# A batch's last pair in the second attention is attended one step later, and its outputs are turned in the next batch's second step

## The reference

```python
q = ln(x @ Wq + bq)                 # 16 heads of 16, 256 queries for each batch
k = ln(y_main @ Wk + bk); v = y_main @ Wv + bv      # 240 keys
k_dca, v_dca = ...                  # 16 more keys, from other weights
ctx = softmax(q k^T / 4) v + softmax(q k_dca^T / 4) v_dca   # two softmaxes, added
x = x + tanh(g_xattn[2]) * (ctx @ Wo + bo)
```

## Time and profile before

| | |
|---|---|
| median of three runs | 1056.01 us |
| the profiled execution | 1059.89 us |
| its span, first to last instruction | 1058.6 us |
| TensorE busy | 936.7 us (88%) |
| VectorE busy | 725.1 us (68%) |
| ScalarE busy | 520.7 us (49%) |
| GpSimd busy | 302.5 us (29%) |
| the steps of the second attention | about 705 to 867 us of the span |

### The profile page before, as it was taken

How to read it: one execution, slowest core, us unless ns; L and a number is a source line. 1 busy time by engine, 2 the same in 40 slices (tenths; PEclk the granted TensorE clock), 3 DMA queues, 4 the chain that set the end, 5 groups by cost and what they waited for, 6 DMA issues and landing times.

```text
span 1058.6 us, 14861 instructions
## 1 busy us (share of the span) xinstructions
PE 936.7 (88%) x4790; PEld 669.3 (63%) x4790; DVE 725.1 (68%) x1877; ACT 520.7 (49%) x1346; POOL 302.5 (29%) x284
## 2 busy tenths in 40 slices
PE   7878789999999999999999989877589988979667
PEld 3323334567999998888977767754355655545455
DVE  5899894245777677678676445576978965576764
ACT  4665672135666666566653434354346552123331
POOL 3767692121111112155101324234232200010210
PEclk8878899999999999999999999999899999989789
DMA  9500001001111164113103446312100003211201
GB/s 363 228 0 0 1 0 50 1 30 45 35 41 46 45 236 153 31 62 94 46 1 119 147 133 191 128 65 60 51 1 1 2 1 141 78 46 31 87 1 41
DMA packets 28500, 75.00 MB, mean 71 GB/s; under 512 B 4092, under 2 KB 5382, under 8 KB 27656
## 3 DMA queue, kind: packets, MB, share of 16 engines
q1 hardware_dynamic: 24344, 63.81, 17.6%
q0 software_dynamic: 3072, 8.39, 2.5%
q10 hardware_dynamic: 1008, 1.86, 0.6%
HBM read 52.03 MB, written 22.02 MB: 70 GB/s over the span
## 4 chain that ended last, share of the span: by engine, by line
PE 62%; DVE 15%; ACT 3%; issue 3%; DMA 1%; SPq 1%; POOL 1%; another core or an unknown queue 0%; DVEq 0%; POOLq 0%; ACTq 0%
PE psum L2195 5%; PE psum L1071 5%; PE psum L1796 5%; PE psum L1277 4%; PE psum L1288 4%; PE psum L927 4%; PE psum L1257 4%; PE psum L1268 2%; PE psum L938 2%; PE psum L1810 2%; PE psum L1095 2%; PE psum L2214 2%; PE psum L2816 2%; PE psum L2458 2%; DVE arena L2492 2%
## 5 line engine op out<-in xcount | busy, mean ns | idle before, releaser
L1167 POOL TENSOR_TENSOR arena<-arena,mhalf 128x8 f32<-128x8 f32 x32 | 53.4, 1670 | 232.6 <-DVE arena L1144 232.6
L1389 DVE SCALAR_TENSOR_TENSOR X<-psum,arena,X 128x256 f32<-128x256 f32 x128 | 56.0, 479 | 64.9 <-PE psum L1288 64.9
L455 POOL TENSOR_TENSOR arena<-arena 128x512 f32<-128x512 f32 x64 | 82.2, 1307 | 8.6 <-PE psum L545 5.1
L855 DVE TENSOR_TENSOR_SCAN arena<-psum,arena 128x512 f32<-128x512 f32 x64 | 74.8, 1210 | 7.9 <-ACT psum L711 6.8
L1331 ACT ACTIVATE arena<-psum,arena 128x256 f32<-128x256 f32 x128 | 59.9, 477 | 35.9 <-DVE arena L1368 33.5
L1796 PE MATMUL psum<-arena 128*128 x248 | 66.6, 391 | 10.6 <-DVE arena L1891 8.8
L2477 ACT ACTIVATE arena<-psum,arena 128x240 f32<-128x240 f32 x128 | 57.4, 463 | 32.3 <-DVE arena L2491 16.4
L545 PE MATMUL psum<-arena,ident 128*128 128x512 f32 x128 | 69.4, 669 | 0.1
L1288 PE MATMUL psum<-arena 128*128 128x256 f32 x256 | 65.9, 380 | 1.2 <-DVE X L1389 1.1
L1257 PE MATMUL psum<-arena 128*128 128x256 f32 x256 | 65.8, 380 | 0.0
L1277 PE MATMUL psum<-arena 128*128 128x256 f32 x256 | 65.8, 380 | 0.0
(11 more groups left out here) (367 smaller groups left out, 2255.7 us busy)
## 6 DMA issues: line engine op xcount, KB each, us to landing
arena<-in_w SPq DMA_DIRECT2D x32, 384.0 KB, 3.1
tokens<-arena SPq DMA_DIRECT2D x2, 4096.0 KB, 22.8
arena<-tokens SPq DMA_DIRECT2D x32, 256.0 KB
results<-arena SPq DMA_DIRECT2D x32, 256.0 KB
arena<-in_moe SPq DMA_DIRECT2D x17, 384.0 KB, 3.1
arena<-in_moe SPq DMA_DIRECT2D x4, 1536.0 KB, 12.8
arena<-in_w SPq DMA_DIRECT2D x2, 1024.0 KB, 6.1
arena<-in_gu SPq DMA_DIRECT2D x1, 1280.0 KB, 7.2
```

The costliest lines, as they stand in the source:

```text
L455: nc.gpsimd.tensor_tensor(m.HC[:, v, :], m.Hs[:, v, :], m.Cs[:, s % 2, :], ALU.mult).then_inc(*tick("HC", s, c))
L855: nc.vector.tensor_tensor_scan(m.Hs[:, 2 * (s % 2) + c, :], bank[m.bank_dA[c]], input_of(m, s, c), 0.0, ALU.mult, ALU.add).then_inc(*tick( ...
```

## The change

The loops are reordered around a batch's end. `attend(s - 1)` now runs in every step but the first, and never twice; only the very last pair is attended after the loop. The copies OSa and OSv move from g = 7 to the next batch's g = 0, behind PTa and PTv (on VectorE ahead of the maxima). `turned` moves from g = 0 to g = 1 and stands ahead of the scores; `normalised` moves to g = 1, ahead of the maxima; its reader's additions on GpSimd move to g = 1, `out_transposed` and its copy to g = 3, `project` to g = 4. The reciprocal of a later batch's first pair is computed in the second step, since `normalised` still reads the old ones.

```diff
 TensorE
         transposed(s)
+        if b and g == 1:
+            turned(b - 1)
         if s + 2 < B * STEPS:
             a2_scores_pe(k, m, s + 2)
-        if b and g == 0:
-            turned(b - 1)
-        elif b and g == 2:
+        if b and g == 3:
             out_transposed(b - 1)
-        elif b and g == 3:
+        elif b and g == 4:
             project(b - 1)
-        if g:
+        if s:
             attend(s - 1)
-        if g == STEPS - 1:
-            attend(s)
         for _ in range(2 if s < 12 else 1):
             step(beside[s // 16])
+    attend(B * STEPS - 1)
 ScalarE, behind the copy PTa
-        if b and g == 2:
+        if b and g == 0:
+            attended(b - 1)
+        elif b and g == 3:
             out_act(k, m, b - 1)
-        if g == STEPS - 1:
-            (wait for a2_AV of s; copy OSa)
+        if s == B * STEPS - 1:
+            attended(b)
 VectorE, behind the copy PTv
+        if b and g == 0:
+            attended(b - 1)
+        elif b and g == 1:
+            normalised(b - 1)
         if s + 2 < B * STEPS:
             a2_maxima_dve(k, m, s + 2)
-        if b and g == 0:
-            normalised(b - 1)
-        elif b and g == 3:
+        if b and g == 4:
             project(b - 1)
-        (reciprocal of s)
-        if g == STEPS - 1:
-            (wait for a2_AV of s; copy OSv)
+        if b and g == 1:
+            inverse(s - 1)
+        if g or not b:
+            inverse(s)
+        if s == B * STEPS - 1:
+            attended(b)
 GpSimd
-        if b and g == 0:
+        if b and g == 1:
             (the two additions for out_transposed(b - 1))
```

More of the change, by code:

```diff
@@ L2897, in attention2_act, with attended @@
     STEPS, KM = m.STEPS, m.KM
+    def attended(b):
+        act.wait_ge(*at("a2_AV", STEPS * b + STEPS - 1))
+        if b:
+            act.wait_ge(*at("a2_OSr", b - 1))
+        nc.scalar.copy(m.OS[:, 0:2, :], bank[6].rearrange("p (q t) -> p q t", q=2)).then_inc(*tick("a2_OSa", b))
     for s in range(B * STEPS):
@@ L2952, in project, with attended, inverse @@
             deviation_dve(k, "m2", b // 2)
+    def attended(b):
+        dve.wait_ge(*at("a2_AV", STEPS * b + STEPS - 1))
+        if b:
+            dve.wait_ge(*at("a2_OSr", b - 1))
+        nc.vector.tensor_copy(m.OS[:, 2:4, :], bank[7].rearrange("p (q t) -> p q t", q=2)).then_inc(*tick("a2_OSv", b))
+    def inverse(s):
+        b, g = s // STEPS, s % STEPS
+        dve.wait_ge(*at("a2_sum", s))
+        if b:
+            dve.wait_ge(*at("a2_O", b - 1, 1))
+        nc.vector.reciprocal(m.inv[:, :, pair_places(g)[2], :],
+                             m.sums[:, :, pair_places(g)[2], :]).then_inc(*tick("a2_inv", s))
     for s in range(B * STEPS):
```

## The result

| | before | after |
|---|---|---|
| median of six runs each, us | 1057.26 (1054.38 to 1060.22) | 1065.82 (1064.23 to 1066.56) |
| the profiled execution, us | 1059.89 | 1064.56 |
| its span, us | 1058.6 | 1063.3 |

A forecast was written before the change was run, and what follows sets the result against it. TensorE, busy 936.7 of 1058.6 us, was taken as the bound, its holes set by VectorE's queue. Terms +1.3, -1.5, -0.7, +2.6 gave +1.7, plus 0.3 for the clock: +2.0, median 1056.01 to 1058.0 us, range 1051.5 to 1064.5.

The forecast's parts named there:

- What bounds the kernel: Whole kernel: TensorE busy 936.7 of 1058.6 us, so time is saved only where it idles or runs at half clock.
- the price of the split pair: Batch ends: two attends in a row, 1.57 us together, become 2 x 0.98; +0.39 us of TensorE per boundary.
- Batch 1 to 2: Up to T(21): out_transposed's 2.39 us wait becomes four short ones, TensorE at full clock; -1.5 us.
- The charge for the scale operations behind GpSimd's additions: maxima(19) on VectorE: both scale operations meet an addition, +0.35 to +0.45 us each, 0.8 together; bounds 0 and 1.9.
- T(21) to T(24): Late in batch 2: A(22) and A(23) no longer a pair, two waits shrink; -0.7 us, bounds 0 and -1.0.
- Batch 2 to 3: T(24) to T(29): router work delays normalised(2), A(24) waits 2.4 us; +2.6 us, plus 0.3 for a clock fall.
- Batch 0 to 1: Up to T(13): L2722 starts about 0.5 us earlier, project(0) moves to the dense stretch; +1.3, bounds -0.5 and +3.
- the root's chain behind `normalised(0)`: Boundary of batch 0 to 1: the chain feeding L2584 comes about 1.9 us later.
- the signs that the forecast named: A(16), A(24) wait 1.4, 2.4 us; out_transposed 0.5, 1.7; long L2497; project(0) near 790; clock under 0.9 if slow.
- (c): Rival, all three boundaries: A(8b) waits 2.4 us, following steps run at half clock; 1062.5 us, chance 0.16.
- (b): Rival, whole stage: TensorE's holes close and its clock stays full; -6.5 us, 1049.5 us, chance 0.16.
- (d): Rival: A(8b-1) simply moves and VectorE governs everything, within 0.5 us; 1056 us, chance 0.08.

The follow-up runs named there:

- after_again: The kernel after, unchanged, run once more beside the variants of its set: ratio 1.0070 to the kernel before.
- bias_late: The kernel after with GpSimd's bias addition L2789 of batches 2 and 3 three side steps later: ratio 1.0034 to the kernel before.
- early_out: The kernel after with out_transposed and project back at g = 2 and 3: ratio 1.0052 to the kernel before.
- copy_behind: The kernel after with VectorE's OSv behind the maxima of step g = 0 instead of ahead: ratio 0.9997 to the kernel before.
- mended: The kernel after with the edits of copy_behind and bias_late together: ratio 0.9973 to the kernel before.
- last_two: The kernel before with the change at the last two batch boundaries only: ratio 1.0007 to the kernel before.
- pair_g2: The kernel after with A(8b) put off to g = 2, directly ahead of A(8b+1): ratio 1.0065 to the kernel before.
- double_scores: The kernel after with scores S(19) and S(27) issued twice: ratio 1.0067 to the kernel before.
- warm: The kernel after with 12 idle matmuls at the end of step 7 and 12 in step 8: ratio 1.0036 to the kernel before.
- late_out: The kernel before with only out_transposed, its copy and project one step later (g = 3 and 4): ratio 0.9990 to the kernel before.
- late_out_last: The kernel before with out_transposed and project one step later for batches 1 and 2 only: ratio 0.9963 to the kernel before.
- third set: The runs of after_again, copy_behind, mended and late_out_last, compared with runs of the kernel before on the same chip; after_again's ratio there is 1.0070.
- first_only: The kernel before with the change at the boundary of batch 0 to 1 only: ratio 1.0033 to the kernel before.
- router_later: The kernel after with the head of the 8-expert FFN (router) two side steps later on all engines: ratio 1.0038 to the kernel before.
- before_again: The kernel before, unchanged, profiled a second time (the second profile of before): 1059.24 us.

## Why the prediction was wrong

**What bounds the kernel; the price of the split pair.** Right. T(13) to T(16) is 9.27 us after and 9.85 before: A(15) gone from there, 0.58, as in the working.

**Batch 1 to 2, -1.5.** Nearly right. T(13) to T(21) is 30.55 us against 31.65 (second profile), -1.1. All the waits came within 0.1 us: 1.42 (forecast 1.45), 0.33 (0.4), 0.56 (0.5). The charge for the scale operations behind GpSimd's additions, +0.8, was 0.51 + 0.49 (they took 0.68 and 0.66 for 0.17).

**T(21) to T(24), -0.7.** It is -0.2, within the bounds.

**Batch 2 to 3, +2.6 and +0.3 for the clock.** The waits are right (2.37 for 2.4 at A(24)), but out_transposed waits 0.67 and not 1.65. The term that was mis-sized is the clock. Four groups at half clock (2.03 + 1.79 + 1.84 + 2.02 us) lose against 1.13 + 1.06 + 1.09 + 1.13 some 3.3 us, where 0.3 stood. I had weighed only the wait at A(24), as one chance in three, because behind a wait of 2.13 us it had not fallen; that was one profile, and in the second one of before it fell behind the same wait (2.12 us). Both profiles of the kernel after show all four groups slow. The kernel before has some of this as well (clock .92 in its second profile, 1.00 in the first on which the forecast rests), so the loss here is 25.2 less 22.4, 2.8 us, by the second profile and 4.4 by the first. That 2.8 is next to the forecast 2.9 is chance: the clock cost 3.3 and not 0.3, `out_transposed` waited 1.0 less, T(27) not at all in place of 0.4, and the second profile of before had itself lost 1.6 to the clock there. S(26) was slow in six forms with the new order (after, after_again, bias_late, early_out, copy_behind, mended) and fast in four (last_two, pair_g2, double_scores, warm), with the same matmuls and the same hole of 0.38 us ahead of it, and fast in all six profiled forms with the old order there. Which of the falls is due to the wait and which to the narrow matmuls isn't settled.

**Batch 0 to 1, +1.3 (bounds -0.5 and +3).** This is the step that failed. From T(0) to T(13) the kernel after takes 86.5 us and the kernel before 81.2, +5.3. The forecast said that L2722 "starts about 0.5 earlier"; from T(0) it starts 0.96 later (59.01 against 58.05 us). In the words of the prediction VectorE, and with it L2722, "gains only the 0.64 of OSv and gives it back waiting for A(7)": that was half of it, for OSv waited 2.30 us, and behind it a maxima operation lost 1.41 more to L2789. The sentence that hid this was "the side gathers on GpSimd in batch 0 come in the same place". GpSimd runs in order too: the two additions that moved out of step 8 had been what held L2789 back, and nothing in the sum asked what moves *forward* when something ahead of it is moved away. bias_late shows the share of this: 1.4 us of the hole, and 3.4 us from T(8) to T(13) with the clock of L2722, which the kernel after had low in both its profiles (5.38 for 3.69 us) and bias_late had high. The rest lies behind T(9): T(9) to T(13) is 22.24 us against 19.64, +2.6, where about 1.8 stood. Of this the root's chain behind `normalised(0)` makes 2.1, near the forecast 1.9:
```profile
783.97 2.07 POOL L2584 TENSOR_TENSOR arena<-arena 128x512 f32<-128x512 f32 x2 [6.76 <-DVE arena L2978]
```
That is 13.26 us behind T(9), in the kernel before 11.19. The place of `project(0)` makes the other 0.5: early_out, which has it back at g = 3, takes 21.71 us there.

The sum of these terms, forecast against measured: 1.3, -1.5, -0.7, 2.9 against 5.3, -1.1, -0.2, 2.8. It is +2.0 against +6.8, and 4.0 of the 4.8 missing are at the first boundary. Of the signs that the forecast named, the waits of A(16) and A(24), the long L2497 behind `normalised` and `project(0)` at 790.07 came; the clock between 842 and 850 was 0.92, not under 0.9, since the slow groups lay mostly to both sides of it.

**The rule on the shared port.** The Trainium skill (SBUF — State Buffer, Who interferes with whom) says that of a two-port VectorE operation and a GpSimd operation the first to issue holds the pair for its whole instruction and the other is blocked. The measured ends agree to 0.03 us: 763.89 for 763.87 in the kernel after, 766.20 for 766.17 in copy_behind. The rule was in the working, applied to the two additions, which moved, and not to L2789, which nobody moved and which moved all the same; by it alone L2497 would have been charged up to L2789's 2.35 us.

**The rivals.** (c), `normalised` between OSv's wait and A(8b), was given at 1062.5 and is nearest in size. Its mechanism came at the last boundary (2.37 us and half clock behind it), not at the second (1.42 us, clock 1.00); at the first, A(8) waited 0.32, and the loss came another way. (b), faster, fell on VectorE's queue, as pair_g2 shows. A part of (b) was hidden in the change and is the versions late_out and late_out_last: the wait of out_transposed is split over two groups (1.39 and 0.49 for 2.39), with no wait for `normalised` added. (d), no effect within 0.5 us, falls with the time.

**What the first profile hid.** The forecast put T(13) at 792.95, and it is at 792.95. That is chance: the profile of before was 4.3 us long from T(0) to T(8), for the two waits between T(0) and T(3), and the new loss fills that up. Only the distance from a cut close by shows the miss.

**Open.** The medians differ by 8.6 us (7.4 by the third set's ratio, 0.0070 of 1060.66) and the stage by 6.8 in the profiles. The part behind the stage lasts between 189.6 us (early_out, mended, late_out_last) and 192.2, with the same instructions. Cut into stretches of 12 us, mended and after_again differ there in the granted clock: in the second and the sixth stretch it is 1.00 in the short one and 0.86 in the other. What sets it wasn't tried. Part of the low medians of mended and late_out_last may be such a tail: both were profiled with the short one, the second profile of before with 192.0. And the medians of copy_behind and mended (by the ratios 0.3 and 2.9 us under before) don't fit their stages, 4.2 and 2.5 us longer than in the second profile of before.

## What to carry to other kernels

When an instruction is moved on an engine that runs in order, list what stood behind it as well, and follow each of these forward to its new time: an operation let go early can block a tiny one elsewhere. Put a copy that waits for the latest result behind the work that is ready already: moving OSv behind the maxima took A(24)'s wait from 2.37 to 0.54 us. Test each part of a reordering by itself, since the useful half (the reader of a contested bank one step later) can be had without the other, and take two profiles of the kernel before ahead of the sum.

## What the runs showed of the hardware

A VectorE scale operation on 128 x 2 values of 0.17 us took 0.46, 0.68, 1.11, 1.58 and 2.32 us, each time to within 0.03 us of the end of the GpSimd addition that was running, while the reductions and copies of VectorE out of PSUM beside the same additions kept their 0.64 and 0.68 us. What counts is what is left of the GpSimd instruction, and not the length of the small one.

TensorE's clock was at its lower level for most of L2722 (16 matmuls, 5.38 against 3.69 us) behind a hole of 3.59 us in after, after_again, early_out and first_only and of 3.32 in copy_behind, and longer still in router_later (6.35 us behind 3.60). It was at its upper level behind a hole of the same 3.59 us in pair_g2 and double_scores, and behind the holes of 2.20 us and less ahead of L2722 (2.20, 2.17, 2.08, 1.70, 1.27, 1.12). A hole of that length is not safe elsewhere: the groups behind `out_transposed(2)`, which waits 2.12 or 2.13 us in the kernel before, ran at half clock in before_again and first_only and at full clock in the first profile. After the router's 16 matmuls of 8 columns (1.95 us) and a hole of only 0.38 us S(26) ran at 1.2 GHz in the kernel after and at 2.4 GHz in double_scores, where ahead of it only S(19), some 30 us earlier, is doubled. A hole of this size makes a fall possible, not certain. A forecast should carry it as a chance with its price (1.7 us here), and one profile does not tell the price of an edit.
